# Bias rows split in the first stage, a context mask applied by matrix products, and two reorderings in the latent cross-attention

## What is computed

```
# third layer: latents = layernorm(x), 1024 of them; context of 77 keys with a mask
kv   = concatenate([xn_context @ Wkv.T, ln @ Wlkv.T], axis=1)
attn = einsum('bhid,bhjd->bhij', rmsnorm(q) * SCALE, rmsnorm(k))
attn = where(full_mask, attn, -max); attn = softmax(attn)
out  = einsum('bhij,bhjd->bhid', attn, v) @ Wo.T + bo
# fourth layer: h = swiglu((xt @ w1 + b1) * (xt @ w3 + b3)); y = h @ w2 + b2, for 8 experts and a shared one
```

## Time and profile before

| | us |
|---|---|
| median of 3 runs (lowest, highest) | 990.91 (989.98, 994.02) |
| the profiled execution | 988.14 |
| its span, first to last instruction | 986.40 |
| PE, DVE, ACT, POOL busy in it | 882.6, 681.3, 529.3, 408.6 |
| first stage, until POOL's first L595 | 0 to 67.1 |
| steps n = 1 to 6 of the third layer | 265.6 to 483.2 |

### The profile page before, as it was taken

The page is one execution under the profiler, slowest core; times in us unless marked ns, Lnnn a source line. Parts: engine busy times, 40 slices in busy tenths (PEclk is TensorE's granted clock), DMA queues, the critical chain, the costliest instruction groups (busy, mean ns, idle before and its releaser), DMA issues.

```text
span 986.4 us, 15071 instructions
## 1 busy us (share of the span) xinstructions
PE 882.6 (89%) x4259; PEld 616.8 (63%) x4263; DVE 681.3 (69%) x1331; ACT 529.3 (54%) x841; POOL 408.6 (41%) x324
## 2 busy tenths in 40 slices
PE   8975678988999899899989899989999999999991
PEld 4643445554455455455446687777888888888881
DVE  4678987875576886776389677865656666565666
ACT  2436776536566556557653633414556666566650
POOL 1114331645476776866623454631222322222310
PEclk9898988999999999999999999999999999999995
DMA  9300000003676676675683500029650178617315
GB/s 302 92 1 1 0 0 1 1 0 125 270 283 236 249 292 224 250 286 220 260 322 106 213 1 0 2 77 423 227 211 32 37 292 321 266 43 276 96 36 171
DMA packets 49494, 153.97 MB, mean 156 GB/s; under 512 B 6176, under 2 KB 24024, under 8 KB 43822
## 3 DMA queue, kind: packets, MB, share of 16 engines
q1 hardware_dynamic: 45710, 144.17, 39.2%
q0 software_dynamic: 3744, 9.31, 3.0%
HBM read 97.89 MB, written 56.49 MB: 157 GB/s over the span
## 4 chain that ended last, share of the span: by engine, by line
PE 52%; DVE 21%; DMA 10%; issue 6%; ACT 5%; POOL 4%; SPq 1%; DVEq 0%; ACTq 0%; POOLq 0%
PE banks L1007 6%; PE banks L1256 6%; PE banks L1258 6%; PE banks L1257 6%; DMA wsplit<-cv_hl 4%; DMA aux<-moe_x,small 3%; PE banks L976 2%; PE banks L999 2%; PE banks L917 2%; PE banks L1000 2%; PE banks L1281 2%; POOL cv_hl L645 2%; PE banks L1283 1%; PE banks L1282 1%; DMA ring<-wsplit 1%
## 5 line engine op out<-in xcount | busy, mean ns | idle before, releaser
L1007 PE MATMUL banks<-wexp 128*65 128x512 f32 (+1 forms) x288 | 151.1, 606 | 6.8 <-ACT wexp L1542 6.7
L1256 PE MATMUL banks<-ring,x_hi 128*128 x312 | 127.5, 409 | 0.0
L645 POOL TENSOR_TENSOR cv_hl<-wexp,cv_hl 128x1024 fp32r<-128x1024 f32 x45 | 108.5, 2419 | 45.3 <-ACT cv_hl L1519 44.8
L1258 PE MATMUL banks<-ring,x_lo 128*128 x312 | 122.1, 391 | 0.0
L1257 PE MATMUL banks<-ring,x_hi 128*128 x312 | 121.9, 391 | 0.0
L1542 ACT ACTIVATE wexp<-banks 128x512 f32<-128x512 f32 x128 | 76.1, 599 | 59.0 <-PE banks L1000 58.9
L1998 DVE TENSOR_REDUCE small<-banks 128x1 f32<-128x1101 f32 x64 | 83.5, 1304 | 34.8 <-PE banks L976 34.8
L1672 ACT ACTIVATE banks<-wexp 128x1024 f32 x72 | 73.5, 1020 | 47.7 <-DVE aux L2354 47.7
L1655 ACT ACTIVATE aux<-banks 128x512 f32<-128x512 f32 x78 | 46.6, 598 | 62.6 <-PE banks L1258 46.6
L999 PE MATMUL banks<-q_hi,k_hl 128*128 128x512 f32 x144 | 77.4, 537 | 1.7 <-ACT q_lo L1510 1.0
L1519 ACT ACTIVATE cv_hl<-wexp 128x1024 fp32r<-128x1024 f32 x45 | 51.2, 1137 | 35.8 <-DMA wsplit<-cv_hl 35.8
(11 more groups left out here) (358 smaller groups left out, 2262.9 us busy)
## 6 DMA issues: line engine op xcount, KB each, us to landing
wsplit<-cv_hl SPq DMA_DIRECT2D x45, 1024.0 KB, 7.9
ring<-wsplit SPq DMA_DIRECT2D x32, 1280.0 KB, 15.3
wexp<-in_L_ffn_w SPq DMA_DIRECT2D x40, 512.0 KB, 5.9
wexp<-in_expert_biases SPq DMA_DIRECT2D x8, 1152.0 KB, 6.7
ring<-wsplit SPq DMA_DIRECT2D x4, 1024.0 KB, 8.6
wexp<-moe_y SPq DMA_DIRECT2D x8, 512.0 KB, 6.6
wexp<-in_L_ffn_sw SPq DMA_DIRECT2D x5, 512.0 KB, 9.2
x_sb<-in_x SPq DMA_DIRECT2D x4, 512.0 KB, 8.0
```

What stands on the lines that cost most here:

```text
L645: g.tensor_tensor(sides(hl[:, PIECE:2 * PIECE]), raw, sides(hl[:, 0:PIECE]).bitcast(f32), ALU.subtract).then_inc(s['cv_lo'], 1)
L1007: mm(pb[5 + half][0:DA, :], vh[b][0:w, c, :], pT[q % 3][0:w, :], start=c == 0, stop=c == len(KTILES) - 1).then_inc(s['a_pv'], 1)
L1256: mm(o[:], x_hi[u][:, kc, :], hi, start=kc == 0 and not primed, stop=False, skip_group_check=primed)
L1258: last = mm(o[:], x_lo[u][:, kc, :], hi, start=False, stop=primed and kc == KC - 1, skip_group_check=primed)
```

## The change

POOL clears `bias_f` before anything is loaded into it, at the very start, and does the whole split of the bias rows right behind L585, in the first stage, with the 96 x 2304 subtraction cut into three of 96 x 768. `bias_f` and `bias_part` move to the part of memory in which the split pieces lie later. The turning of the context's keys becomes a product with a diagonal matrix that holds the mask, and a second product adds the first key to the masked columns; the two DVE instructions behind `low` go, and `a_khl` with them. The key copy on POOL waits for ACT's roundings alone and stands behind two pieces of the weight split. `maxima` start at unit 5 of a step, one earlier, while `joined` stays where it is.

```diff
+            g.memset(bias_f, 0.0).then_inc(s['r_zero'], 1)
             g.iota(eno_i[:], pattern=[[0, 1]], base=0, channel_multiplier=1).then_inc(s['const'], 1)
...
             link(g.tensor_tensor(wo_2[DH:P], wo_raw[DH:P], wo_2[DH:P].bitcast(f32), ALU.subtract))
+
+            pool.wait_ge(s['ld_route'], NLD['ld_route'])
+            part, third = bias_part[0:96, :], NB // 3
+            for k in range(3):
+                link(g.tensor_copy(part, bias_f[0:96, :]))
+                link(g.tensor_copy(bias_b[32 * k:32 * k + 32, :], part[32 * k:32 * k + 32, :]))
+                for c in range(0, NB, third) if k < 2 else ():
+                    link(g.tensor_tensor(bias_f[0:96, c:c + third], bias_f[0:96, c:c + third], part[:, c:c + third], ALU.subtract))
+            pool.sem_inc(s['r_bias'], 1)
...
-                        if p == 1:
-                            pool.wait_ge(s['a_khl'], n + 3)
+                        if p == 2:
+                            pool.wait_ge(s['a_hi'], 5 * (n + 3))
                             head_keys(b)
...
-                for k in range(PARTS)[i::NH - 1]:
-                    if k == 0:
-                        pool.wait_ge(s['ld_route'], NLD['ld_route'])
-                    link(g.tensor_copy(part, bias_f[0:96, :]))
-                    link(g.tensor_copy(bias_b[32 * k:32 * k + 32, :], part[32 * k:32 * k + 32, :]))
-                    if k < PARTS - 1:
-                        link(g.tensor_tensor(bias_f[0:96, :], bias_f[0:96, :], part, ALU.subtract))
...
-                    last = tr(TP[:, 0:SK], k_dup[0:SK, TB, :], ident[0:SK, 0:SK])
+                    mm(TP[:, 0:SK], k_dup[0:SK, TB, :], mask_ok[0:SK, b, :], start=True, stop=False)
+                    last = mm(TP[:, 0:SK], k_dup[0:1, 0, :], mask_no[0:1, b * SK:(b + 1) * SK], start=False, stop=True)
...
-                lag, head_at = (3, 5) if first else (0, 6)
+                lag, head_at = (3 if first else 0), 5
...
+                for b in range(B):
+                    link(v.tensor_scalar(mask_ok[0:SK, b, :], ident[0:SK, 0:SK], mask_col[:, b:b + 1], None, ALU.mult))
...
-                if k < 4:
-                    last.then_inc(s['t_free'], 1)
-                else:
-                    link(last)
-                    kx, words = k_hl[b][:, at], slice(b * SK, (b + 1) * SK)
-                    link(v.tensor_tensor(kx, kx.bitcast(f32), mask_ok[:, words], ALU.mult))
-                    v.scalar_tensor_tensor(kx, mask_no[:, words], k_hl[b][:, 0:1].bitcast(f32), kx.bitcast(f32), ALU.mult, ALU.add)\
-                        .then_inc(s['t_free'], 1)
-                    ve.wait_ge(s['t_free'], free)
-                    ve.sem_inc(s['a_khl'], 1)
...
-                for t in range(TB):
-                    if not last:
+                for t in range(TB + 1):
+                    if not last and t < TB:
                         maximum(n + 1, t)
...
-                    if not first:
-                        joined(use if last else use + 5, 1 - b, t, last)
+                    if not first and t > 0:
+                        joined(use if last else use + 5, 1 - b, t - 1, last)
```

More of the change, by code:

```diff
@@ L196, in program @@
         scr.take(3 * SLOTS)
-        mask_ok = scr.take(SKB)
-        mask_u = mask_ok.bitcast(i32)
+        mask_ok = scr.take(SKB, B)
+        mask_u = mask_ok.rearrange("p a b -> p (a b)").bitcast(i32)
         first = scr.at
@@ L255, in program @@
         h_moe = gate
-        bias_f = aux[:, 0:NB]
+        bias_f = wexp[:, 0:NB]
+        bias_part = wexp[:, NB:NB + NB // 2].bitcast(bf16)
+        assert NB + NB // 2 <= CVHL * 2 * PIECE
         ident = sb("ident", [P, P])
@@ L649, in _ @@
                 if p == PER_STEP // 2 - 1:
-                    pool.wait_ge(s['a_khl'], 2)
+                    pool.wait_ge(s['a_hi'], 10)
                     head_keys(1)
-            PARTS = 3
-            part = bias_part[0:96, :]
             for i in range(NH - 1):
@@ L1817, in masks @@
                 ve.wait_ge(s['ld_l1'], NLD['ld_l1'])
-                v.tensor_scalar(mask_no, mask_u, -1.0, 1.0, ALU.mult, ALU.add)
-                link(v.tensor_scalar(mask_ok, mask_u, 1.0, None, ALU.mult))
+                link(v.tensor_scalar(mask_no, mask_u, -1.0, 1.0, ALU.mult, ALU.add))
+                link(v.tensor_scalar(mask_col[:], maskc_u[:], 1.0, None, ALU.mult))
+                for b in range(B):
+                    link(v.tensor_scalar(mask_ok[0:SK, b, :], ident[0:SK, 0:SK], mask_col[:, b:b + 1], None, ALU.mult))
                 link(v.tensor_scalar(mask_col[:], maskc_u[:], BIG, -BIG, ALU.mult, ALU.add))
@@ L1973, in _, with low @@
             TURNED = (0, 1, 2, 7, 0)
-            def low(n, b, k, free, o=None):
+            def low(n, b, k, o=None):
                 o = pb[TURNED[k]] if o is None else o
@@ L1983, in low @@
                 at = slice((k % 2) * 512, (k % 2 + 1) * 512) if k < 4 else slice(S, S + SK)
-                last = v.scalar_tensor_tensor(dst[:, at], src[:, 0:at.stop - at.start], gam, hi[:, at].bitcast(f32), ALU.mult, ALU.subtract)
-                if k < 4:
-                    last.then_inc(s['t_free'], 1)
-                else:
-                    link(last)
-                    kx, words = k_hl[b][:, at], slice(b * SK, (b + 1) * SK)
-                    link(v.tensor_tensor(kx, kx.bitcast(f32), mask_ok[:, words], ALU.mult))
-                    v.scalar_tensor_tensor(kx, mask_no[:, words], k_hl[b][:, 0:1].bitcast(f32), kx.bitcast(f32), ALU.mult, ALU.add)\
-                        .then_inc(s['t_free'], 1)
-                    ve.wait_ge(s['t_free'], free)
-                    ve.sem_inc(s['a_khl'], 1)
+                v.scalar_tensor_tensor(dst[:, at], src[:, 0:at.stop - at.start], gam, hi[:, at].bitcast(f32), ALU.mult, ALU.subtract)\
+                    .then_inc(s['t_free'], 1)
             def maximum(n, t, o=0):
@@ L2022, in step @@
                     for k in range(5):
-                        low(n + 1, 1 - b, k, use + 5)
-                for t in range(TB):
-                    if not last:
+                        low(n + 1, 1 - b, k)
+                for t in range(TB + 1):
+                    if not last and t < TB:
                         maximum(n + 1, t)
@@ L2053, in _ @@
                     for k in range(2):
-                        low(0, 0, k, 5, pb[HEAD0_BANK[k]])
+                        low(0, 0, k, pb[HEAD0_BANK[k]])
                 if t == TB + 3:
                     for k in range(2, 5):
-                        low(0, 0, k, 5, pb[HEAD0_BANK[k]])
+                        low(0, 0, k, pb[HEAD0_BANK[k]])
             mean_squares(NSA, NSS, T)
             root_means(NSA, NSS, TB, T)
-            v.tensor_copy(mx4[:, 1:2], f_max[:, 0:1]).then_inc(s['l_free'], 1)
             scaled(0, 1)
```

12 lines of the change are left out of this document (4 added, 8 removed).

## The result

The changed kernel takes 1012.81 us in the median of 6 runs (1005.56 to 1015.49), against 991.06 us for the kernel before, also 6 runs. The ratio is 1.0204, 95% interval 1.017 to 1.0238. The forecast was 993 us, with 983 to 1000 as its range; none of its rivals lay above 997. The profiled execution took 1012.47 us, its span is 1010.7 us: 24.3 us more than the span of 986.4 before. That is 22 us more than forecast.

A forecast was written before the change was run, and what follows sets the result against it. PE, busy for 882.6 of 986.4 us, was taken to bound the kernel, so only its waits or work count. Third layer -10 and first stage +12 sum to +2 us: 993 us, range 983 to 1000.

The forecast's parts named there:

- its rivals: Against 993 us (chance 0.46): first stage loses little, 984, 0.24; first stage loses more, 997, 0.22; third-layer wait stays, 996, 0.08.
- The bias rounds leave the steps: Third layer: steps 3 and 5 fall to the floor of 33.99 us, gaining 4.47 + 5.99 = 10.5 us.
- The key copy: Third layer, steps 2, 4 and 6: second piece ends earlier, gaining 3.2 us, less 1 for a wait that may stay.
- The mask by products: Third layer: two products lose 0.41 us a step, 2.5 in six; 0.95 and 0.6 gained in and before step 0.
- Maxima one unit ahead: Third layer: the first maxima lack a `joined`, PE idles 0.3 us in each of six steps, 1.9 us lost.
- The first stage, +12: First stage: POOL's early bias split takes turns with DVE, delaying two L1796 groups by 10 us, plus 2 for PE's clock.
- the term for the clock: First stage: PE loses its clock while waiting; scores, turning and warming products cost more at 1.2 GHz, 2 us taken.
- The bound of +16: First stage: upper bound of the loss, if both groups run at the low clock; as a rival 997 us, chance 0.22.
- a wait showed up that no row has: Sign that the prediction is wrong: a new wait, for one between the two products and ACT's rounding at unit 5.

The follow-up runs named there:

- the first three experiments: Kernel before with the early bias split alone, 997.01 us; changed kernel with seventh output's addition first on DVE, 992.80; changed kernel with maxima back at unit 6, 989.01.

## Why the prediction was wrong

The forecast was +2 us, not clear of noise; what came was +22, clear of noise and 12.8 us above the range. Of the 20 us between them, most come from one step of the working, the earlier `maxima`, and the rest from the clock behind the first stage.

- **The bias rounds leave the steps, 10.5:** right, 10.4 in the run with this part alone.
- **The key copy, 3.2 less 1:** the wait for L1542 went, but by the mask's move and not by the place (0.4). As a set, with the bias rounds and the products, they were priced within 2 us: 217.66 - 10.5 - 3.2 + 1 + 2.5 = 207.5 forecast for the six steps without the earlier maxima, 205.67 measured. The place alone costs 6.7 us.
- **The mask by products:** 0.41 a step forecast, 0.4 measured; 1.55 forecast up to the end of step 0, 1.9 measured.
- **Maxima one unit ahead: the step that failed.** The prediction priced it with "PE idles 0.3 us in each of six steps: 1.9 us lost", and went on that "Step 1 shows no wait before `minus` either, so nothing is gained". The 0.3 was right (0.26). What it left out is the seventh output on DVE. It looked at what PE does in the unit that loses its `joined`, the first, and not at the last, which has a `joined` and no maxima; and it named no queue behind the eighth maximum and the negation, though they now stand ahead of an addition that frees a bank. The trace of before had the numbers: 1.30 for the maximum, 0.33 for the negation, 0.64 for the addition behind it, and 1.33 us of PE work in a unit without maxima. The maximum gives 0.3 us of wait, as the run with the negation behind the output shows, and the negation at its old length would give 0.3 more. The other 1.5 us of the 2.1 a step are the turn with POOL's sixth piece: the negation's new time (310.2) lies in it, the old one at its very end. With PE's longer work, at a lower clock in two of the steps, this wait cost 17.2 us, and the whole reordering 18.7 where 1.9 was forecast (224.38 against 205.67).
- **The first stage, +12:** the taking of turns and its price were right: in the first three experiments both groups meet POOL, 6.73 and 5.92 us, 6.78 and 5.14, 6.65 and 5.38. That this trace shows 12.7 at L595 is partly luck, since only its first group waited (5.8 us) and PE's clock and a late start made up for the second. Too small was the term for the clock: 2 us, where the low level came a second time and reached into the second layer for another 5.7. The prediction had put the stage's end at POOL's first L595 and priced nothing behind it. In the four traces with the early split in large pieces and the first layer's order unchanged (the changed kernel and the first three experiments) the loss up to the fourth L1438 is 18.4, 16.8, 18.7 and 13.2 us, and 21.5 in the long execution (1003.42 us) of the run with the negation behind the seventh output. These are differences to one trace. The seven traces without the early split have that landmark at 86.5 to 94.3 us, 89.0 in the median, and 86.91 is one of the earliest: the loss is there in all, but its size is known to a few us only.
- **The bound of +16** was thus too low by up to 2.7 us in those four, when it is held against the fourth L1438, and there was no rival in which a part of the third layer went wrong by a new wait. The forecast had said that it would be wrong if a wait showed up that no row has, and had looked for it between the products and ACT's rounding.

Not settled is why PE's clock comes back in one execution and not in the next of the same program: the same kernel before ran from 982.64 to 1005.85 us in these series, and traces with the same first stage (100.14, 105.29, 105.60) differ by up to 5.5 us at the fourth L1438. No run here separates it from the order of the work.

## What to carry to other kernels

When one of two interleaved sequences is shifted against the other, walk through both ends of the overlap, not only the one that changes: ask at the last unit which buffer the remaining sequence needs, and what now stands ahead of its release on the engine that frees it. An instruction that is moved in time meets other instructions of the engine with which it takes turns; read what runs on that engine at the new time. And a wait on an engine can protect another: POOL's standing still for the mask was what let the mask run, so edits that were priced one by one have to be tried in pairs.

## What the runs showed of the hardware

- DVE's instructions differ in whether they wait for POOL. The negation, from SBUF to SBUF with 8 elements a partition, took 1.41 us instead of 0.17 to 0.33, the mask's second instruction, with two operands in SBUF, 2.33 instead of 0.30 in the kernel before; the additions that read one operand from PSUM (L2002, 0.48) and the maxima out of PSUM (1.30) kept their length beside POOL's pieces, as L1991 at 308.85 beside the piece at 309.17. The Trainium skill, SBUF — State Buffer, section "Who interferes with whom", says that an instruction of DVE with at most one input in SBUF doesn't contend unless it runs in a two-port mode, which tensor_scalar can enter, and that one with two inputs in SBUF does. These rows agree with it, though none shows the negation's mode. The forecast knew the lock, and didn't ask it about the negation.
- The length of an idle time of PE doesn't tell whether its clock falls. Ahead of the eighth output it was idle for 1.79, 2.18, 2.45, 2.52, 1.77 and 1.78 us in steps 1 to 6; the step's granted clock was 0.96 in the third and the sixth, and 1.00 in the fourth, which had the longest.
- Cutting POOL's instructions to ninths brought the wait of a group of four from 5.8 to 0.8 us over its length, and stretched POOL's work on the split from 23 to 38 us, first to last instruction.
